# Expert choice: a threshold search on one transposed matrix with three bits a level, one rank pass, and another order of weight loads

## The reference

```python
logits = xf @ Wr + br
Sm = jax.nn.softmax(logits, axis=-1)
G_t, idx_t = jax.lax.top_k(Sm.T, k)          # k = 2048 // 8 = 256
tokens = xf[idx]
mid = jax.nn.silu(jnp.einsum('keh,ehf->kef', tokens, Wu) + bu)   # F = 682, W_up shared by two experts
out = jnp.einsum('kef,efh->keh', mid, W_down) + b_down
y = jnp.zeros_like(xf).at[idx].add(G[..., None] * out)
x = x + jnp.tanh(g_ffn[1]) * y
```

## Time and profile before

| what | us |
|---|---|
| median of three runs (876.07 to 879.52) | 878.72 |
| span of the profiled execution | 879.3 |
| time of the profiled execution beside its span | none is given |
| last stage begins (first copy, `spread`) | 716.24 |
| first count of the search | 726.08 |
| end of the search (`thr_row`) | 753.21 |
| `at_lo` of expert 0 | 760.60 |

### The profile page before, as it was taken

One profiled execution on the slowest core, in us unless ns is written; L12 is line 12 of the kernel. 1 busy time (PEld: TensorE's weight loads), 2 busy tenths in 40 slices (PEclk: granted clock), 3 DMA queues, 4 the chain that ended last, 5 costly groups with the idle time before them and its releaser, 6 DMA issues. The chain is left out here.

```text
span 879.3 us, 14726 instructions
## 1 busy us (share of the span) xinstructions
PE 642.7 (73%) x4856; PEld 476.7 (54%) x4856; DVE 512.7 (58%) x1634; ACT 415.4 (47%) x810; POOL 343.0 (39%) x474
## 2 busy tenths in 40 slices
PE   3988898288999999999124868877779630168794
PEld 2777786157767777877112445554445420046673
DVE  1477656655665566554015577777873438866562
ACT  1354431174685577556111556655656311056571
POOL 2233333376336434742212435434443130124553
PEclk9999999679999999999655789898888755579997
DMA  5253223256354435431211222231200122025542
GB/s 186 74 181 97 73 92 125 67 154 158 89 126 108 134 85 141 108 67 19 48 42 40 61 61 86 75 81 57 74 26 27 40 83 83 8 67 133 141 106 31
DMA packets 73871, 75.93 MB, mean 86 GB/s; under 512 B 8037, under 2 KB 66449, under 8 KB 73553
## 3 DMA queue, kind: packets, MB, share of 16 engines
q1 hardware_dynamic: 61217, 59.32, 21.4%
q0 software_dynamic: 10928, 15.57, 10.2%
q10 hardware_dynamic: 1664, 0.27, 0.2%
HBM read 52.20 MB, written 22.94 MB: 85 GB/s over the span
## 5 line engine op out<-in xcount | busy, mean ns | idle before, releaser
L1866 DVE CUSTOM_DVE_ANT_0 c_sn<-c_ps_s,k_mask 128x128 f32<-128x128 f32 (+1 forms) x256 | 75.8, 352 | 55.5 <-PE c_ps_s L2004 55.4
L1390 PE MATMUL b_ps_y<-b_w2h,b_hh 128*128 128x256 f16 x320 | 87.3, 273 | 6.4 <-DVE b_xl L1283 4.4
L1390 PE MATMUL b_ps_y<-b_w2h,b_hl 128*128 128x256 f16 x320 | 87.2, 273 | 0.0
L1390 PE MATMUL b_ps_y<-b_w2l,b_hh 128*128 128x256 f16 x320 | 87.2, 273 | 0.0
L1698 POOL TENSOR_SCALAR_AFFINE_SELECT c_pr<-c_pr 128x512 f32<-128x512 f32 x64 | 43.1, 674 | 112.9 <-ACT c_pr L1757 111.9
L1200 POOL DMA_INDIRECT res<-b_y,b_s_idx x40 | 69.3, 1732 | 41.8 <-ACT b_y L1242 33.4
L1274 DVE TENSOR_TENSOR b_hl<-b_h,b_hh 128x640 f16<-128x640 f32 x64 | 52.8, 825 | 38.6 <-ACT b_hh L1222 36.6
L1186 POOL DMA_INDIRECT e_xg<-rows,e_g_idx x35 | 38.2, 1093 | 87.9 <-DVE e_g_idx L1301 73.8
L2032 PE MATMUL c_ps_v<-c_pr,k_vx 128*64 128x256 f32 (+1 forms) x512 | 64.2, 378 | 5.4 <-POOL c_pr L1698 4.8
L1757 ACT ACTIVATE c_pr<-c_ps_t 128x768 f32<-128x768 f32 x64 | 51.7, 808 | 16.0 <-PE c_ps_t L2018 16.0
L1355 PE MATMUL b_ps_h<-b_xh,e_w1h 128*128 128x320 f16 x256 | 56.9, 304 | 2.7 <-ACT b_h L1217 1.6
(11 more groups left out here) (409 smaller groups left out, 1762.5 us busy)
## 6 DMA issues: line engine op xcount, KB each, us to landing
e_w<-in_L_ffn_W_dram SPq DMA_DIRECT2D x16, 1024.0 KB
d_w<-in_L_ffn_W_down_dram SPq DMA_DIRECT2D x8, 640.0 KB
k_ks<-kT SPq DMA_DIRECT2D x48, 64.0 KB, 2.7
c_qs<-q SPq DMA_DIRECT2D x48, 64.0 KB, 2.3
d_w<-in_L_ffn_W_up_dram SPq DMA_DIRECT2D x4, 682.0 KB, 5.8
rows<-a_rows SPq DMA_DIRECT2D x8, 264.0 KB, 2.6
rows<-c_rows SPq DMA_DIRECT2D x8, 264.0 KB, 2.2
a_x_in<-in_x_dram SPq DMA_DIRECT2D x8, 256.0 KB, 3.1
```

Of the source, the lines that this page charges most:

```text
L1390: last = pe.matmul(ps_y[(j + CT) % 2][:, 0:D], a, b[:, f, :], start=(f == 0 and k == 0), stop=(f == FC - 1 and k == 2))
L1866: dve.tensor_tensor_reduce(sn[r][:, a:b], ps_s[:, r, a:b], mask[:, a:b], -1.0, 3.0e38, ALU.add, ALU.min, mx[g % 2][:, q, r, j:j + 1]).then ...
```

## The change

`byexp` is now one 128x128 transpose of `prob`: partition 8i + e holds the 128 probabilities that token tile i has for expert e. A level settles three bits with seven candidates, which are seven columns: seven counts of 128 elements each write one column of `cnt`, and one product with `same` (now built from `expert_of` and `own`) adds the columns over the 16 partitions of an expert. There are ten levels. `ok` compares and sums over the seven columns in one operation; `base`, the candidates without this level's bits, is made while TensorE works.

There is one rank pass: `above` and `tied` are each scanned and multiplied once, written at an offset of one column in `flat` so that the scan is exclusive, and the slot follows from both ranks (`less`, `short`, `fits`, `slot`, `hi16`, `lo16`). `both`, `taken` and `value` are made on GpSimd, and VectorE waits for `value` in `marked(0)`. The transpose of `bu_in` moves behind the fifth level and its copy `buT` into the seventh. SP issues the loads of `w1` for groups 2 and 3 before the loads of `w2` for experts 3 and 5.

The diff, cut to its core; of the search loop and the ranks only the added lines and some that frame them are shown:

```diff
-    GRP = P // E
-    LEVELS = [26, 22, 18, 14, 10, 6, 2, 0]
+    BITS = 3
+    TRIES = (1 << BITS) - 1
+    LEVELS = list(range(30 - BITS, -1, -BITS))
...
-        spread = sb("spread", [P, NT, E, GRP])
-        byexp = sb("byexp", [P, N])
+        byexp = sb("byexp", [P, P])
...
+            sp.wait_ge(s_wl1, 1)
+            load_up(1)
             for e in range(E):
-                if e % 2 == 0 and group(e) + 1 < G:
-                    sp.wait_ge(s_wl1, group(e) + 1)
-                    load_up(group(e) + 1)
                 if e + 2 < E:
                     sp.wait_ge(s_wl2, e + 1)
                     load_down(e + 2)
+                if e % 2 == 0 and group(e) + 2 < G:
+                    sp.wait_ge(s_wl1, group(e) + 2)
+                    load_up(group(e) + 2)
...
+            pool.iota(expert_of[:], pattern=[[0, NT], [1, E]], base=0, channel_multiplier=0,
+                      allow_small_or_imprecise_dtypes=True).then_inc(s_cst, 1)
+            pool.iota(lane_i[:], pattern=[[0, 1]], base=0, channel_multiplier=1).then_inc(s_cst, 1)
+            pool.iota(try_i[:], pattern=[[1, TRIES]], base=1, channel_multiplier=0).then_inc(s_cst, 1)
...
+            pool.wait_ge(s_fits, 1)
+            pool.tensor_tensor(both[:], fits[:], tied, ALU.mult).then_inc(s_both, 1)
+            pool.wait_ge(s_both, 1)
+            pool.tensor_tensor(taken[:], both[:], above, ALU.add).then_inc(s_taken, 1)
+            pool.wait_ge(s_taken, 1)
+            pool.tensor_tensor(value[:], token1[:].unsqueeze(1).to_broadcast([P, E, NT]), taken[:], ALU.mult)\
+                .then_inc(s_value, 1)
...
-            act.wait_ge(s_pt, 2)
-            for k in (1, 3):
-                act.wait_ge(s_pt, k + 1)
-                act.activation(byexp[:, k * 512:(k + 1) * 512], ps_t[:, k, :], ACT.Copy).then_inc(s_byA, 1)
...
+            dve.tensor_scalar(own_i[:], lane_i[:], E - 1, None, ALU.bitwise_and).then_inc(s_try, 1)
             for n, low in enumerate(LEVELS):
                 if low:
-                    dve.tensor_scalar(tries[:, n:n + 1], try_i[:], low, None, ALU.logical_shift_left)\
+                    dve.tensor_scalar(tries[:, n, :], try_i[:], low, None, ALU.logical_shift_left)\
                         .then_inc(s_tries, 1)
                 else:
-                    dve.tensor_scalar(tries[:, n:n + 1], try_i[:], 2, None, ALU.logical_shift_right)\
-                        .then_inc(s_tries, 1)
-            for k in (0, 2):
-                dve.wait_ge(s_pt, k + 1)
-                dve.tensor_copy(byexp[:, k * 512:(k + 1) * 512], ps_t[:, k, :]).then_inc(s_bye, 1)
-            dve.wait_ge(s_pbu, 1)
-            dve.tensor_copy(buT[:], ps_i[:, 0:FC * G]).then_inc(s_buT, 1)
-            dve.wait_ge(s_bye, 2)
-            dve.wait_ge(s_byA, 2)
+                    dve.tensor_copy(tries[:, n, :], try_i[:]).then_inc(s_tries, 1)
+            dve.wait_ge(s_try, 1)
+            dve.tensor_copy(own[:], own_i[:]).then_inc(s_own, 1)
+            dve.wait_ge(s_pt, 1)
+            dve.tensor_copy(byexp[:], ps_t[:, 0, 0:P]).then_inc(s_bye, 1)
+            dve.wait_ge(s_own, 1)
+            dve.tensor_scalar(same[:], expert_of[:], own[:, 0:1], None, ALU.is_equal).then_inc(s_same, 1)
+            dve.wait_ge(s_bye, 1)
...
             for n, low in enumerate(LEVELS):
+                at = tries[:, 0, :] if n == 0 else cand[:]
+                if n:
+                    dve.wait_ge(s_cand, n)
+                for j in range(TRIES):
+                    dve.tensor_scalar(hit[:, j, :], byexp[:], at[:, j:j + 1].bitcast(F32), 0.0, ALU.is_ge, ALU.add,
+                                      accum_out=cnt[:, j:j + 1]).then_inc(s_cnt, 1)
+                if n == 1:
+                    dve.tensor_copy(thr[:], more[:]).then_inc(s_thr, 1)
+                elif n:
+                    dve.tensor_tensor(thr[:], thr[:], more[:], ALU.bitwise_or).then_inc(s_thr, 1)
+                if n and low:
                     dve.wait_ge(s_thr, n)
+                    dve.tensor_tensor(base[:], tries[:, n + 1, :], thr[:].to_broadcast([P, TRIES]), ALU.bitwise_or)\
+                        .then_inc(s_base, 1)
+                if n == 6:
+                    dve.wait_ge(s_pbu, 1)
+                    dve.tensor_copy(buT[:], ps_i[:, 0:FC * G]).then_inc(s_buT, 1)
                 dve.wait_ge(s_pok, n + 1)
+                dve.tensor_scalar(ok[:], ps_r[:, 0:TRIES], float(TAKE), 0.0, ALU.is_ge, ALU.add,
+                                  accum_out=level[:]).then_inc(s_level, 1)
+                dve.wait_ge(s_level, n + 1)
+                dve.tensor_scalar(more[:], level[:], float(1 << low), None, ALU.mult).then_inc(s_more, 1)
+                dve.wait_ge(s_more, n + 1)
                 if low:
+                    count(dve, s_base, n)
+                    start = base[:] if n else tries[:, 1, :]
+                    dve.tensor_tensor(cand[:], start, more[:].to_broadcast([P, TRIES]), ALU.bitwise_or)\
+                        .then_inc(s_cand, 1)
+            dve.wait_ge(s_thr, len(LEVELS) - 1)
+            dve.tensor_tensor(thr[:], thr[:], more[:], ALU.bitwise_or).then_inc(s_thr, 1)
             dve.wait_ge(s_thr, len(LEVELS))
...
+            dve.tensor_tensor(above, by_e, bt, ALU.is_gt).then_inc(s_cmp, 1)
+            dve.tensor_tensor(tied, by_e, bt, ALU.is_equal).then_inc(s_cmp, 1)
+            for k in range(2):
+                dve.wait_ge(s_cmp, 2 - k)
+                dve.tensor_tensor_scan(wide(excl[k]), flat[k][:, 0:E * NT], wide(run_on), 0.0, ALU.add, ALU.mult)\
+                    .then_inc(s_excl, 1)
+            def ranks(k):
+                return ps_t[:, 1 + k, 0:E * NT].rearrange("p (e i) -> p e i", e=E)
+            dve.wait_ge(s_prank, 1)
+            dve.tensor_reduce(less[:], ranks(2), AX_X, ALU.add, negate=True).then_inc(s_less, 1)
+            dve.wait_ge(s_less, 1)
+            dve.wait_ge(s_prank, 2)
+            room = less[:].unsqueeze(2).to_broadcast([P, E, NT])
+            dve.scalar_tensor_tensor(out=short[:], in0=ranks(0), scalar=-float(TAKE), in1=room, op0=ALU.add,
+                                     op1=ALU.min).then_inc(s_short, 1)
+            dve.scalar_tensor_tensor(out=fits[:], in0=ranks(0), scalar=-float(TAKE), in1=room, op0=ALU.add,
+                                     op1=ALU.is_le).then_inc(s_fits, 1)
+            dve.wait_ge(s_short, 1)
+            dve.wait_ge(s_prank, 3)
+            dve.scalar_tensor_tensor(out=slot[:], in0=short[:], scalar=float(TAKE - 1), in1=ranks(1), op0=ALU.add,
+                                     op1=ALU.add).then_inc(s_slot, 1)
+            dve.tensor_scalar(hi16[:], slot[:], float(P), None, ALU.is_ge).then_inc(s_hi, 1)
+            dve.wait_ge(s_hi, 1)
+            dve.scalar_tensor_tensor(out=lo16[:], in0=hi16[:], scalar=-float(P), in1=slot[:], op0=ALU.mult,
+                                     op1=ALU.add).then_inc(s_lo, 1)
+            dve.wait_ge(s_lo, 1)
...
+                if e == 0:
+                    dve.wait_ge(s_value, 1)
...
-            pe.wait_ge(s_spr, 1)
-            for i in range(NT):
-                last = pe.transpose(ps_t[:, i // 4, (i % 4) * P:(i % 4 + 1) * P],
-                                    spread[:, i, :, :].rearrange("p e j -> p (e j)"), ident[:])
-                if i % 4 == 3:
-                    last.then_inc(s_pt, 1)
-            pe.wait_ge(s_ldb, 48)
-            pe.transpose(ps_i[:, 0:FC * G], bu_in[:], ident[0:FC * G, 0:FC * G]).then_inc(s_pbu, 1)
-            pe.wait_ge(s_cst, 12)
+            pe.transpose(ps_t[:, 0, 0:P], prob[:].rearrange("p i e -> p (i e)"), ident[:]).then_inc(s_pt, 1)
+            pe.wait_ge(s_same, 1)
             for n in range(len(LEVELS)):
-                pe.wait_ge(s_ok, n + 1)
-                pe.matmul(ps_r[:, 0:1], same[:], ok[:], start=True, stop=True).then_inc(s_pok, 1)
+                pe.wait_ge(s_cnt, (n + 1) * TRIES)
+                pe.matmul(ps_r[:, 0:TRIES], same[:], cnt[:], start=True, stop=True).then_inc(s_pok, 1)
+                if n == 4:
+                    pe.wait_ge(s_ldb, 48)
+                    pe.transpose(ps_i[:, 0:FC * G], bu_in[:], ident[0:FC * G, 0:FC * G]).then_inc(s_pbu, 1)
-            pe.wait_ge(s_abv, 1)
-            pe.matmul(ps_r[:, 256:256 + E * NT], ones16[:], wide(marks[2]), start=True, stop=True)
+            pe.wait_ge(s_cst, 13)
+            pe.wait_ge(s_cmp, 2)
+            pe.matmul(ps_t[:, 3, 0:E * NT], ones16[:], flat[1][:, 1:1 + E * NT], start=True, stop=True)\
+                .then_inc(s_prank, 1)
             for k in range(2):
-                pe.wait_ge(s_in, k + 1)
-                if k:
-                    pe.wait_ge(s_fits, 1)
-                pe.matmul(ps_r[:, 0:E * NT], tri[:], wide(marks[k]), start=True, stop=False)
+                out_k = ps_t[:, 1 + k, 0:E * NT]
+                pe.matmul(out_k, tri[:], flat[k][:, 1:1 + E * NT], start=True, stop=False)
-                pe.matmul(ps_r[:, 0:E * NT], ones16[:], wide(excl[k]), start=False, stop=True).then_inc(s_prank, 1)
```

(45 more changed lines are left out.)

76 lines of the change are left out of this document (11 added, 65 removed).

## The result

The changed kernel takes 863.79 us (median of four runs, 862.95 to 864.36) against 877.39 us before in the same comparison: ratio 0.9851, 95% interval 0.9814 to 0.9887, a gain of 13.6 us. 861.6 was forecast from a median of 878.72, a gain of 17.1. The time lies in the stated range of 856 to 870, in the upper half of the forecast's own case (858.8 to 865.5); the gain is four fifths of the one forecast.

A forecast was written before the change was run, and what follows sets the result against it. The last stage was taken as bound by its serial head before expert 0 and ScalarE's waits for `w1`. Gains of 10.1 and 7.0 us, together 17.1, took the median from 878.7 to 861.6 us, range 856 to 870.

The forecast's parts named there:

- The search: Last stage, threshold search: ten levels of 2.85 us make 28.6 us against 27.1 before, so 1.5 us more.
- c: Search: distance from one count's start to the next's, taken as 0.27 us, between 0.22 and 0.43.
- Rival (a): Search: short counts do not overlap, distance 0.35 to 0.43 us, losing 4.8 to 9.6 us; chance 0.16.
- the exception that the prediction names: Search: the Trainium skill's exception to its drain rule, for two Vector instructions with no wait between them.
- The head before the search: Start of the last stage: first count comes after 1.6 us instead of 9.8, with 0.6 for ten shifts.
- Two of my own signs: Last stage: first count within 3 us of its start, and `at_lo` of expert 0 some 34 us in.
- Rank and slots: From `thr_row` to expert 0's `at_lo`: 1.0 us stays, then 3.05 us instead of 6.4, gaining 3.35.
- The cover of `value`: Before `vhi` of expert 0: `at_lo` and `at_hi` hide GpSimd's products of 1.0 to 2.0 us; failing costs up to 0.5.
- The loads: Expert loop: earlier third and fourth `w1` loads end both ScalarE waits, gaining 7.0 us, between 0 and 9.5.
- Rival (b): Expert loop: early `w1` loads share transfer engines, TensorE waits for rows instead, no gain, up to 868.6 us; chance 0.13.
- case (e): Whole kernel: the forecast itself, 858.8 to 865.5 us, with the iota bound in it; chance 0.57.
- the head's 10.1: Last stage up to `at_lo` of expert 0: 34.3 us instead of 44.4, so 10.1 us earlier.

The follow-up runs named there:

- two_bits: The changed kernel with two bits a level, 15 levels of three counts each, instead of three bits: 861.1 us, ratio 0.9849 to the kernel before.
- fill_late: The changed kernel with GpSimd's zero fills of the `w2` buffers held back until VectorE has made `tries`: 865.0 us, ratio 0.9867 to the kernel before.
- small_fill: The changed kernel with GpSimd zeroing only the last 256 of 1536 columns of each `w2` buffer: 862.0 us, ratio 0.9832 to the kernel before.
- loads_only: The kernel before with only SP's new order of `w1` loads: 869.7 us, ratio 0.9931 to the kernel before.
- old_order: The changed kernel with SP's old order of loads put back: 869.7 us, ratio 0.9915 to the kernel before.
- value_dve: The changed kernel with `both`, `taken` and `value` made on VectorE ahead of `slot`, not GpSimd: 865.1 us, ratio 0.9883 to the kernel before.

## Why the prediction was right, and where it was off

**The search.** Right in kind and in size: c = 0.27 us from the overlap in the earlier trace rows, a level 2.84 for 2.85, and the search 1.3 us longer than before. Rival (a) falls: each of the 60 counts that follow another in its level starts before that one has ended, beside its accumulator read. The rule of the Trainium skill behind it (VectorE: DVE Perf Modes, "The DRAIN you can't avoid") is not borne out by these counts, which fall under the exception that the prediction names. `two_bits` shows the same two constants at another number of counts. The advice to minimise the number of operations still has a true core here, as each start costs 0.27 us for 0.13 of work, and going from seven to three starts a level paid although it made five more levels.

**The head before the search.** This is the step that failed: "Then ten shifts: [...] so 0.6 [...] In all 1.6 us". It measured 4.45. The term was sized from small operations that ran alone, and I named GpSimd's order but not that its fills, 2.7 us long, would lie beside these shifts. The trace of before had the sign of it, a copy of 4.62 us in which more than half the time was the same stall, and I took its whole length as removed. `fill_late` and `small_fill` show the cause, and with the fills away the first count comes at 1.72 us. Two of my own signs failed with it: the first count did not come within 3 us, and `at_lo` stood at 37.2 us and not at some 34. No rival named this loss, and its 2.85 us are more than twice the 1.2 that I kept as the bound for the iotas, which were in fact quick (0.12 and 0.13 us). That the time still fell into the range is luck in part: the range was made wide for other causes.

**Rank and slots.** 4.3 us for 4.04; the 0.27 missing are `lo16` beside GpSimd, 0.16, and small change. The cover of `value` held with 2.3 us to spare.

**The loads.** The forecast was 7.0. The two places themselves gave 6.5 in `loads_only` and 7.2 in `old_order` against the changed kernel. Rival (b) falls: no new TensorE wait on `xg` appeared. The number is right, the account of it only in part: I priced it by how much earlier ScalarE ends `y`, while TensorE waited for `h` only 4.5 us in all, and the rest of the gain is mostly the clock, 1.4 us for each place where it had fallen behind the wait. The sum has no term for that, so part of the agreement is luck. What the forecast also lacked is that the rest moves by more than 2 us with the clock's rise, whatever the change.

**The sum.** 17.1 forecast; less 2.85 for the stall and 0.27 in the ranks leaves 14.0, near the measured 13.6 (14.8 by the stretches; in them the clock's earlier rise is worth 0.7, as from expert 0's `xh` to expert 1's it was 8.1 us instead of 8.8). The forecast's case (e), 858.8 to 865.5, is what happened, with the head's 10.1 being 7.2.

## What to carry to other kernels

A chain of short operations is priced by the distance between starts, not by their length; look for any pair without a wait in the trace, and then choose the number of candidates by the sum of starts and round trips rather than by the fewest levels. Before booking a slow operation's whole length as a gain, ask whether it was slow by itself or stood still for a neighbour, since the stall stays behind and falls on the next. A wait that leaves TensorE idle can cost more than its length, when the clock falls behind it. A load that frees its buffer early should not stand in the queue behind one whose buffer is freed late.

## What the hardware showed beyond that

**GpSimd's fill stops VectorE.** A fill of 2.7 us (two of 128x1536 float32) held VectorE for about its whole length: int32 shifts by 2.8 us, a float32 copy by about 2.7 (the estimate above), the float16 comparison `same` by 2.5. Fills of 0.55 us held the shifts for 0.6. The Trainium skill (GPSIMD Engine Reference, "1. Specifications") names contention with VectorE instructions in a 2-port mode or with two SBUF inputs; the trace agrees that they contend. It cannot tell whether more is held than this names: the counts of `fill_late`, with one tensor input, ended late too, but they stood behind `same`. What in the fill holds VectorE was not tried. GpSimd's products with two inputs cost far less, 0.16 us on `lo16` and 0.2 on `at_lo`.

**When the clock rises.** Expert 0's first products ran at the lower of TensorE's two levels in every profile, 1.2 GHz, and rose to 2.4 after 2.9 to 5.9 us of them, with TensorE almost idle through the whole head before them (5.8 us busy in the 48 us ahead of 764 in the changed kernel). The stretches by window (busy us and count by engine, then the granted clock), the 6 us from the first product on, of the changed kernel and of `loads_only`:

```profile
765.30:771.30 6.00, 5.96 (x40) 4.49 (x41) 3.72 (x5) 3.59 (x8) 0.00 (x0) 0.75 0.01 3
```

```profile
766.80:772.80 6.00, 6.00 (x30) 4.26 (x30) 3.08 (x4) 2.72 (x6) 0.00 (x0) 0.51 0.01 3
```

40 products against 30 in the same time, at a mean granted clock of 0.75 and 0.51 of full speed. The rest follows it: at 2.9 and 3.3 us it was 111.1 and 111.2, at 4.2 and 4.8 us 112.0 and 112.5, at 5.7 and 5.9 us 113.3 to 113.7. The three latest rises went with a second loss. In `loads_only`, `fill_late` and `value_dve` the clock fell back to the lower level at the rows of expert 2, behind a TensorE wait of 2.3 us for them, and from the `xh` of expert 2 to that of expert 3 it was 10.8 to 10.9 us at a mean of 0.90, where six other executions took 9.9 at 1.00. The changed kernel had the same wait of 2.3 us and its clock stayed up. (The kernel before took 10.7 us there at 1.00, which is not explained.)

What sets the moment of the rise or the fall stays open. Together they make a spread of 2.6 us in kernels whose instructions there are all but the same, which is more than most single edits here.
